# Last feed-forward in pairs of tiles, interleaved with the attention steps, in a two-layer gated block on one core

## What is computed

```python
x = x + tanh(g_xattn[0]) * attention_0(layernorm(x), ctx)         # stage A, one head
x = x + tanh(g_ffn[0])   * quantised_ffn_0(layernorm(x))          # stage B
# stage C, attention of 16 heads of 16 columns
q, k, v = layernorm(x) @ Wq.T + bq, ctx @ Wk.T + bk, ctx @ Wv.T + bv
probs = softmax(clip(mask(q @ k.T / 4), -50, 50))
delta = clip(residual_scale, 0, 0.3) * ((probs @ v) @ Wo.T + bo)
x = x + tanh(g_xattn[1]) * ((delta - mean) / sqrt(var + 1e-5) * ln_gamma + ln_beta)
# stage D, the last feed-forward, 256 -> 1024 -> 256
h = layernorm(x)
x = x + tanh(g_ffn[1]) * ((silu(h @ w_gate.T) * (h @ w_up.T)) @ w_down.T)
```

## Time and profile before

| | us |
|---|---|
| median of 3 runs (264.17 to 264.46) | 264.27 |
| the profiled execution | 264.11 |
| its span, first to last instruction | 262.3 |
| TensorE busy in it | 212.0 |
| VectorE busy | 181.0 |
| ScalarE busy | 132.8 |
| GpSimd busy | 83.9 |

### The profile page before, as it was taken

How to read it: one execution, slowest core, us unless ns; L and a number is a source line. 1 busy time by engine, 2 the same in 40 slices (tenths; PEclk the granted TensorE clock), 3 DMA queues, 4 the chain that set the end, 5 groups by cost and what they waited for, 6 DMA issues and landing times.

```text
span 262.3 us, 4538 instructions
## 1 busy us (share of the span) xinstructions
PE 212.0 (81%) x1658; PEld 174.5 (67%) x1658; DVE 181.0 (69%) x457; ACT 132.8 (51%) x296; POOL 83.9 (32%) x108
## 2 busy tenths in 40 slices
PE   0285557979889889897798688775999999999992
PEld 0264325858778778786576466654877888888882
DVE  2769879598988988786428999998984333262333
ACT  1138874478667667679755455553322323222220
POOL 2301111175856856868505333442100000000000
PEclk9999955699999999999959999997999999999999
DMA  5999003900000000000000000000000000020002
GB/s 169 369 390 301 5 0 139 343 1 0 2 0 0 2 1 0 2 2 0 0 2 2 0 2 4 0 4 0 2 2 0 0 0 2 0 80 2 0 0 80
DMA packets 9238, 12.55 MB, mean 48 GB/s; under 512 B 1025, under 2 KB 7937, under 8 KB 9217
## 3 DMA queue, kind: packets, MB, share of 16 engines
q1 hardware_dynamic: 8784, 12.07, 13.3%
q10 hardware_dynamic: 432, 0.20, 0.4%
HBM read 11.22 MB, written 1.05 MB: 47 GB/s over the span
## 4 chain that ended last, share of the span: by engine, by line
PE 50%; DVE 27%; ACT 7%; DMA 6%; issue 4%; POOL 3%; SPq 1%; DVEq 0%; ACTq 0%; POOLq 0%
PE PB L1259 16%; PE PB L1278 7%; DMA WRAW<-w_dram 6%; PE PB L1073 6%; PE PB L1172 4%; PE PB L1085 3%; DVE XV L524 3%; PE PB L1108 2%; PE PB L1112 2%; DVE HBQ L742 2%; PE PB L1019 2%; DVE RD L728 2%; DVE HBQ L572 2%; ACT SIL L906 2%; DVE HSD L578 2%
## 5 line engine op out<-in xcount | busy, mean ns | idle before, releaser
L1259 PE MATMUL PB<-SGN,WHI 128*128 128x512 f32 x128 | 40.5, 397 | 0.0
L1073 PE MATMUL PB<-SGN,XQH 128*128 128x512 f32 x64 | 27.7, 433 | 1.3 <-DVE XQL L553 1.3
L699 DVE TENSOR_TENSOR WRAW<-WRAW,PB 128x512 f32<-128x512 f32 x16 | 11.0, 686 | 24.0 <-ACT WRAW L993 23.9
L1278 PE MATMUL PB<-WHI,SGN 128*128 128x256 f32 x128 | 25.6, 283 | 2.2 <-DVE SGN L707 1.8
L1073 PE MATMUL PB<-SGN,XQL 128*128 128x512 f32 x64 | 27.1, 424 | 0.0
L289 POOL TENSOR_TENSOR RSTD<-MVS,MHALF 128x1 f32<-128x1 f32 x24 | 13.4, 560 | 40.9 <-DVE MVS L401 40.9
L1259 PEld LDWEIGHTS PB<-SGN,WHI 128*128 128x128 f32 x128 | 22.9, 188 | 4.5 <-issue 0.2
L1259 PE MATMUL PB<-SGN,WLO 128*128 128x512 f32 x64 | 25.2, 394 | 0.0
L993 ACT ACTIVATE WRAW<-PB 128x512 f32<-128x512 f32 x16 | 9.6, 600 | 28.0 <-PE PB L1259 28.0
L1278 PEld LDWEIGHTS PB<-WHI,SGN 128*128 128x128 f32 x128 | 20.7, 188 | 3.6 <-DVE SGN L707 2.4
L316 POOL TENSOR_TENSOR HBQ<-HBQ,HR 128x512 f32<-128x512 f32 x16 | 17.6, 1098 | 17.2 <-DVE HR L590 17.2
(11 more groups left out here) (122 smaller groups left out, 545.7 us busy)
## 6 DMA issues: line engine op xcount, KB each, us to landing
WRAW<-w_dram SPq DMA_DIRECT2D x2, 2048.0 KB, 12.1
X<-x_dram SPq DMA_DIRECT2D x2, 512.0 KB, 5.8
CTXT<-ctxt_dram SPq DMA_DIRECT2D x1, 1024.0 KB, 9.6
CTX<-ctx_dram SPq DMA_DIRECT2D x1, 1024.0 KB, 12.0
WRAW<-w_dram SPq DMA_DIRECT2D x1, 1024.0 KB, 14.9
WQK<-wqkvo_dram SPq DMA_DIRECT2D x1, 1024.0 KB, 7.8
WRAW<-wd_dram SPq DMA_DIRECT2D x1, 1024.0 KB, 10.1
out_dram<-X SPq DMA_DIRECT2D x4, 256.0 KB, 2.2
```

Source lines behind the costliest of these rows:

```text
L1073: mm = nc.tensor.matmul(PB[2 * half + m][:], part[:, p, c, :], sgn(m, c, a, b), start=(c == 0 and k == 0), stop=(c == DC - 1 and k == 1))
L1259: mm = nc.tensor.matmul(PB[2 * b + m][:], wcol(w_part, m, c, j), act_part[:, c, g * TG:(g + 1) * TG], start=(c == 0 and i == 0), stop=(c = ...
L1278: mm = nc.tensor.matmul(down_bank(g, k), act_part[:, b, ts], wdown(w_part, j), start=(j == 0 and i == 0 and k % 2 == 0), stop=(j == FC - 1 ...
```

## The change

1. Stage D works on pairs of tiles: TG = 256, NG = 4 groups, 32 units instead of 16. A unit's gate and up are 12 matmuls of 256 columns and share one bank; its down is 6 matmuls of 256 columns into PB[7].
2. Its units stand inside the steps of stage C, four a step from step 3 on (unit 0 is in step 3, unit 17 in step 7, and steps 8 to 11 hold the others). Up to unit 16 all units use one bank, PB[6], so `gate_up_d(n)` waits for the product `gu_d(n-1)`; after it PB[6] and PB[0] alternate.
3. Denominators and values of a tile now both lie in PB[5], and the one signal `c_pv` comes after the values. The reciprocal waits for it.
4. The output bias is a matmul with one row (`ONES[0:1, :]` by `BO`) into the bank that Wo adds to. The statistics and D2 read that bank directly; the scale moves into GAM and into the variance (RES2). `DL` is gone.
5. VectorE's order in a step changes: the statistics of tile t-2, its update, `norm_d` and `lo_d` stand ahead of the reciprocal of tile t-1. Before, that reciprocal was the first instruction of the step.
6. ScalarE switches between the tables of Exp and Silu (`warm`) in each step from 3 to 6. The exponentials of tile t+1 are taken in step t, after `q_out`.
7. The final update is one instruction of 512 columns for two tiles.

The core of the diff:

```diff
-TG = 512
-NG = NT * P // TG
-TPG = TG // P
+TPG = 2
+TG = TPG * P
+NG = NT // TPG
+NB = 4
+SPT = NG * FC // NT
+LEAD = 14
+LAST = (LEAD + NG * FC) // SPT + 1
...
+        def gu_bank(n):
+            return PB[6] if n <= SPT * NT // 2 or n % 2 == 0 else PB[0]
...
             def step_c(t, p):            # VectorE, after
+                n = SPT * t - LEAD
+                if live(t - 2):
+                    dve.wait_ge(c_dl, t - 1)
+                    nc.vector.bn_stats(ST2[:], PB[5][:, 0:D]).then_inc(c_st, 1)
...
+                if ffn(n - 1):
+                    gu_d(n - 1)
...
+                if ffn(n):
+                    gu_d(n)
+                if live(t - 2):
+                    norm_d(t - 2)
...
+                if live(t - 2):
+                    lo_d(t - 2)
                 if live(t + 2):
                     norm(t + 2, p, 2)
+                if ffn(n + 1):
+                    gu_d(n + 1)
+                if live(t - 1):
+                    dve.wait_ge(c_pv, t)
+                    nc.vector.reciprocal(RD[:], PB[5][:, 0:D]).then_inc(c_rd, 1)
...
             def step_c(t, p):            # ScalarE, after
+                n = SPT * t - LEAD
+                switch = ffn(n + 3) and live(t + 1)
                 if live(t + 1):
                     q_out(t + 1)
...
+                if ffn(n + 2):
+                    silu_d(n + 2)
+                if switch:
+                    warm(ACT.Exp)
+                if live(t + 1):
+                    exp_c(t + 1, 1 - p, 0)
...
+                if switch:
+                    warm(ACT.Silu)
+                if ffn(n + 3):
+                    silu_d(n + 3)
+                    hi_gu(n + 3)
...
+            def delta(u):                # TensorE, after
+                pe.wait_ge(c_o, u + 1)
+                nc.tensor.matmul(PB[5][:, 0:D], ONES[0:1, :], BO[:], start=True, stop=False)
+                for c in range(DC):
+                    mm = nc.tensor.matmul(PB[5][:, 0:D], OT[:, c * P:(c + 1) * P],
+                                          WQK[:, 3, c, :], start=False, stop=(c == DC - 1))
+                mm.then_inc(c_dl, 1)
...
             def step_c(t, p):            # TensorE, after
+                n = SPT * t - LEAD
+                if t < NT and ffn(n - 3):
+                    down_d(n - 3)
                 if live(t + 1):
                     q(t + 1, 1 - p)
...
+                if t < NT and ffn(n - 2):
+                    down_d(n - 2)
+                if t == NT:
+                    down_d(n - 3)
+                if ffn(n):
+                    gate_up_d(n)
+                if t >= NT:
+                    down_d(n - 2)
+                if live(t - 1):
+                    head_sums(t - 1, 1 - p)
+                    if not ffn(n):
+                        head_values(t - 1, 1 - p)
+                if live(t - 2):
+                    xd_t(t - 2)
+                if ffn(n + 1):
+                    gate_up_d(n + 1)
+                if live(t - 1) and ffn(n):
+                    head_values(t - 1, 1 - p)
+                if ffn(n - 1):
+                    down_d(n - 1)
+                if ffn(n + 2):
+                    gate_up_d(n + 2)
                 if live(t + 1):
                     scores(t + 1, 1 - p)
                 if live(t + 2):
                     xt_c(t + 2, p)
+                if t >= NT:
+                    down_d(n)
+                if ffn(n + 3):
+                    gate_up_d(n + 3)
+                if live(t - 1):
+                    delta(t - 1)
+                if t < NT and ffn(n):
+                    down_d(n)
+                if t >= NT:
+                    down_d(n + 1)
```

More of the change, by code:

```diff
@@ L790, in _ @@
-            gu_d(1)
-            lo_gu(1)
-            norm_d(NT - 1)
-            for n in range(2, NG * FC):
-                gu_d(n)
-                lo_gu(n)
-                if n == 2:
-                    lo_d(NT - 1)
-                if n >= FC and n % FC == 1:
-                    update_d(n // FC - 1)
+                if ffn(n + 2):
+                    lo_gu(n + 2)
+            for t in range(LAST):
+                step_c(t, t % 2)
             update_d(NG - 1)
@@ L973, in step_c @@
                 if live(t + 1):
                     q_out(t + 1)
-                if live(t):
-                    exp_c(t, p, 2)
-                    exp_c(t, p, 3)
+                if ffn(n):
+                    silu_d(n)
+                    hi_gu(n)
+                if live(t - 2):
+                    hi_d(t - 2)
+                if ffn(n + 1):
+                    silu_d(n + 1)
+                    hi_gu(n + 1)
+                if switch and not ffn(n + 2 - SPT):
+                    warm(ACT.Silu)
@@ L999, in _ @@
[L999 to L1009 removed]
+            for b in range(4):
+                exp_c(0, 0, b)
+            for t in range(LAST):
+                step_c(t, t % 2)
         @block.tensor
@@ L1163, in q, with heads @@
                 mm.then_inc(c_q, 1)
-            def heads(bank, parts, p):
+            def heads(at, parts, p):
                 for c in range(DC):
@@ new lines, in down_d @@
+            def down_d(n):
+                g, j = n // FC, n % FC
+                pe.wait_ge(d_gl, n + 1)
+                if j == 0:
+                    need(pe, d_x, g)
+                for k in range(TPG):
+                    ts = slice(k * P, (k + 1) * P)
+                    terms = ((GUH, WHI), (GUH, WLO), (GUL, WHI))
+                    for i, (act_part, w_part) in enumerate(terms):
+                        mm = nc.tensor.matmul(
+                            PB[7][:, k * D:(k + 1) * D], act_part[:, n % NB, ts],
+                            wdown(w_part, j), start=(j == 0 and i == 0 and k == 0),
+                            stop=(j == FC - 1 and i == 2), skip_group_check=True)
+                mm.then_inc(d_dn, 1)
```

274 lines of the change are left out of this document (111 added, 163 removed).

## The result

The changed kernel takes **268.41 us** (median of four, 267.26 to 269.86); the kernel before, beside it, 264.37. The ratio is 1.0153, 95% interval 1.0095 to 1.0212: slower. A second series beside other kernels gave 267.78 and 1.0137 (1.0107 to 1.0167). The forecast was 266.4, range 260.5 to 269.8, with slower as the likeliest side. Times in this text are medians of all executions, while the ratios compare mean times without the executions that lie more than 1.5% above the fastest of their kernel, so the two can differ by some tenths of a per cent.

A forecast was written before the change was run, and what follows sets the result against it. It took VectorE to bound stage C and TensorE stage D. Steps summed to 263.8 us profiled; 2.5 for clock falls made 266.3, and the median's 0.16 made 266.4, range 260.5 to 269.8.

The forecast's parts named there:

- Early steps: Stage C steps 1 to 3: the loop becomes serial, 8.9 us a step against 7.2; gate-up 0 ends at 156.4.
- the walk: The step-by-step sum with the clock up: last update at 259.4, 263.8 us profiled; rated 0.24 for 263.2 to 265.2.
- A full step: Steps with four units: TensorE work 14.1 us, some 0.2 for changing matmul kinds, 14.9 in all with waits.
- The rest: After step 6's third gate-up: 52.1 us of TensorE work plus waits, kind changes, drain and last update, 58.3.
- The clock: Steps 1 to 3: idle TensorE drops to 1.2 GHz, adding 2.5 us (0 to 6); 265.2 to 269, chance 0.38.
- the signs that were named for "wrong": Clock 1.0 from 140 us or early steps under 8.5 (under 264); product waits behind loads over 0.5 a step (over 267).
- The bias row: Output projection: one more matmul costs TensorE 0.48 us, VectorE loses DL's 0.48, so the exchange is nil.
- The table loads: Full steps: ScalarE's two switches of 1.53 us each are hidden by TensorE's work, with nothing to spare.
- The split: Feed-forward at 256 columns costs nothing (gate-up 1.41, down 0.70); rival that it costs TensorE, 286 to 308: 0.02.
- the clock staying up: Rival: TensorE stays at 2.4 GHz and the summed times hold, 263.2 to 265.2 us; chance 0.24.
- faster: Rival: the fall at 131.9 us goes away too, saving 2.8 us, 261.0; range 259.5 to 263.2, chance 0.28.
- ScalarE as the bound: Rival: dearer table switches add to each of three full steps twice; 267 to 272 with unseen waits, chance 0.08.

The follow-up runs named there:

- e12: The changed kernel as it is, measured once more in a second series: 267.78 us, ratio 1.0137 to the kernel before.
- e9: Changed kernel with the output bias added on VectorE into SBUF and statistics read there, as before; pairs alone: 268.23 us, ratio 1.0153 to the kernel before.
- e6: Kernel before with only the output bias as a one-row matmul and its statistics read from PSUM: 266.96 us, ratio 1.0111.
- e2: Changed kernel without the one-row bias matmul, so the output lacks the bias: 264.58 us, ratio 1.0008 to the kernel before.
- e4: Changed kernel with exp in place of silu and nine table loads fewer, so another output: 266.03 us, ratio 1.0084 to the kernel before.
- e5: Changed kernel with step 2 alone in the order of the kernel before: 266.18 us, ratio 1.0061 to the kernel before.
- e10: Pairs alone (e9) with TensorE's gaps in steps 0 to 3 filled by matmuls nobody reads: 267.81 us, ratio 1.0118 to the kernel before.
- e7: Kernel before with matmuls nobody reads in TensorE's gaps of steps 0 and 7: 262.19 us, ratio 0.9925.
- e8: Changed kernel with bias on VectorE, early gaps filled, step 2 in old order, later XD transposes from step 4: 262.47 us, ratio 0.9931 to the kernel before.

## Why the prediction was right on the side and 1.4 to 2.0 us short

- **Early steps** (forecast 8.9 us a step, gate-up 0 done at 156.4): the mechanism is as described, each link of the chain is there, but the loop is 9.8. The largest parts of the 0.9: the update of X waits for the root and ends 0.8 behind D2 instead of 0.5, `norm_d` takes 0.54 instead of 0.4, projection and drain 1.8 instead of 1.6. The first projection itself came sooner than in the walk (138.74 against 139.4), since the heads of tile 0 ran at the high clock in e12, 1.93 for the 3.6 that were put down. Gate-up 0 took 1.70 and ends at 157.64 in e12, and at 159.3 in the first profile, with the clock. The comparison with 7.2 was off too: this early interval, from the heads of tile 1 to those of tile 2, was 8.0 in before, so the serial loop costs 1.8 here.
- **A full step** (forecast 14.9): 15.3, 15.5 and 15.8 by the ends of the third gate-ups (157.64 for gate-up 0, then 172.93, 188.42, 204.22 in e12, against 171.3, 186.2, 201.1). **This is the term that was mis-sized.** TensorE's work was put at 14.1 and 0.2 for changing kinds; the first profile has 15.50 busy in 15.79. The same step in the chain of e12:

```profile
188.42 1.08 PE PB L1203 x16
...
189.87 1.43 PE PB L1248 x12
191.30 0.62 PE PB L1220 x2
191.92 1.06 PE PB L1222 x4
...
198.99 0.44 PE PB L1033 x2
...
201.87 0.90 PE PB L1264 x6
```

The parts, from end to end as the chain has them: the projection 1.68 instead of 1.45 (the bias row 0.62, the Wo pair 1.06); the first down behind the heads 0.90 instead of 0.70; gate-ups 1.43 to 1.45 instead of 1.41; scores and transposes 1.45 instead of 1.25; the transposes of XD 0.44 for 0.15. The forecast counted from start to start. Counted so, the same step (181.88 to 197.67 in e12) has 6.29 for the gate-ups instead of 5.64, 3.21 for the downs instead of 2.81, 1.08 for the sums instead of 0.87, 1.10 for the query instead of 0.9 (0.81 in the step before), and 1.40 for the projection, which is not over its 1.45. So what is shown is the excess at the changes of kind, 1.4 us in all against 0.2; which kind it is put down to depends on the counting, and no run varied the order of the kinds, so this is read from the traces and not tested. Durations read inside a row of like instructions were too short for pieces that alternate. The wait for `norm_d`, put at 0.5, is 0.24.
- **The rest** (58.3): 59.6 in both profiles. The waits are smaller than forecast, 3.3 us in e12 instead of 4.4 (those of 1.2 and 1.4 for XD are 0.94 and 1.47), so TensorE's work and its seams took 2.4 more.
- So the walk's last update at 259.4 comes at 263.8 in e12: **4.4 us short**.
- **The clock** (2.5 us on top): the new fall came where it was expected, in step 2, behind a stretch with VectorE's reciprocal in it, and cost 1.6 there; in e12 it did not come, and filling the gaps won 0.6 to 1.2 us at the median. The term was over-sized by half or more, and hid part of the walk's error: 266.3 was two errors that half cancel. The side was luck in part as well. The walk alone stood at 263.8, no change, and "slower" came from the clock term; measured, the clock is the small part, and the walk's own terms make the kernel slower with the clock up. Of the signs that were named for "wrong", the first, a granted clock of 1.0 from 140 us on, is there in e12, but at 268.20 us and not under 264. That the old fall ahead of stage D goes was seen in all profiles of kernels in pairs and is in the walk.
- **The bias row** (0.48 for 0.48 on VectorE, nil): nil in before's step, as said, and nil between e9 and e12 within their intervals. What the forecast missed is the end of the loop, where both the row and the longer hold of PB[5] lie on the path: 2 us in e6, and 0.8 of e2's gain.
- **The table loads** (hidden, with nothing to spare): true in columns 4 and 5; 0.9 and 0.5 us were on the path in columns 3 and 6 (e4). The Trainium skill, "ScalarE: Activation LUTs", section "What ACT_TABLE_LOAD costs", states 2.66 us for a switch with its drain; here each took 1.48, and no drain shows.
- **The split** (free): twelve matmuls of 256 columns took 1.43 to 1.45, against 2.80 for 512: 2 to 4% over half; what it adds besides is more changes of kind. The Trainium skill, "TensorE: Matmul & The Clock Gate", section "Back-to-back issue gap", gives 81 ns at 128 columns and 131 at 512 for a sustained stream; by a line between them, an estimate, the split would have cost 22 us. The rows here have 119 ns at 256 columns and 233 at 512.
- **The rivals**: the clock staying up did happen in e12, but not the 263.2 to 265.2 that went with it; faster is excluded; ScalarE as the bound gave a range that holds the result, though e4 finds only 2 us of it there.

What stays open: the source of e5's gain, why e10's median lies so far over its profile, and why the executions of one kernel differ in where the clock falls.

## What to carry to other kernels

When work is interleaved to fill one engine's idle time, price what alternates from rows in which it alternates: a tenth of a microsecond or so at each change of kind made over 1 us of a 15 us step here. Ask where the filler starts: the 13 us of idle time were real, but the loop that runs before any feed-forward is ready became serial and 1.8 us longer (9.8 against 8.0), and that sits wholly on the path. And before moving work to fill gaps, try filling them with nothing: seventeen idle matmuls ahead of two waits were worth 2 us, as much as the whole interleaving at its best, which had its gaps filled too (e7 beside e8).

## What the runs showed of the hardware

- A matmul of one row by 256 columns, two instructions in the trace, took 0.62 us from its start to the next one's, more than each of the 128-row Wo matmuls behind it (0.78 to 0.97 for two, start to start, in e12).
- The stretches of low clock move between executions of one kernel: in step 2 of the changed kernel it was 0.51 in one profile and 1.00 in the other, with the same instructions ahead. On one chip the mean clock of e12's six executions ran from 0.942 to 0.955. Over its 71 executions beside the experiments the kernel before ranged from 262.60 to 266.66 us.
- Where TensorE's idle time was filled with matmuls that nobody reads, the granted clock of what followed was higher: 1.00 from 130 to 140 us in e7's profile against 0.66 in that of before, and a mean over the span of 0.948 to 0.974 in e7's twelve executions against 0.921 to 0.952 in the 29 of before beside them.
